# The adapter's first products of three tiles as split f16 parts, placed three steps later

## The reference, cut to what matters

```python
g = jnp.einsum('bsd,edf->ebsf', h, Wg)
u = jnp.einsum('bsd,edf->ebsf', h, Wu)
expert_outs = jnp.einsum('ebsf,efd->ebsd', jax.nn.silu(g) * u, Wd)
...
x = x + moe
h = jax.nn.relu(jnp.einsum('bsh,bha->bsa', x, w1) + b1)     # a = 32
adapted = jnp.einsum('bsa,bah->bsh', h, w2) + b2
out = x + layernorm(x + adapted) * gamma + beta
```

## Time and profile before

| | |
|---|---|
| median of 3 runs | 297.31 us (297.27 to 297.92) |
| profiled execution, its own time | 297.04 us |
| its span, first to last instruction | 295.2 us |
| PE busy / DVE busy / ACT busy | 290.1 / 268.8 / 231.1 us |
| granted TensorE clock, mean | 0.999 |

### The profile page before, as it was taken

The page is one execution under the profiler, slowest core; times in us unless marked ns, Lnnn a source line. Parts: engine busy times, 40 slices in busy tenths (PEclk is TensorE's granted clock), DMA queues, the critical chain, the costliest instruction groups (busy, mean ns, idle before and its releaser), DMA issues.

```text
span 295.2 us, 5086 instructions
## 1 busy us (share of the span) xinstructions
PE 290.1 (98%) x1510; PEld 144.3 (49%) x1510; DVE 268.8 (91%) x585; ACT 231.1 (78%) x517; POOL 19.3 (7%) x32
## 2 busy tenths in 40 slices
PE   8999999999999999999999999999999999999995
PEld 2444444444444444444444444444444444588883
DVE  5999999998989898988989999999999999977795
ACT  6998878788878787877897788887878876667771
POOL 3200201100000000000002010001100011000011
PEclk9999999999999999999999999999999999999999
DMA  6973110244000000000011001010001110000001
GB/s 208 385 307 109 52 65 19 62 120 112 2 2 0 0 2 0 0 2 1 1 22 26 18 9 39 12 25 19 17 3 39 27 18 10 2 36 3 0 2 36
DMA packets 17940, 13.39 MB, mean 45 GB/s; under 512 B 11486, under 2 KB 15994, under 8 KB 17914
## 3 DMA queue, kind: packets, MB, share of 16 engines
q1 hardware_dynamic: 17482, 12.86, 14.4%
q10 hardware_dynamic: 432, 0.21, 0.2%
HBM read 11.23 MB, written 1.05 MB: 42 GB/s over the span
## 4 chain that ended last, share of the span: by engine, by line
PE 94%; DVE 2%; DMA 1%; SPq 1%; issue 1%; ACT 0%; POOL 0%; POOLq 0%; DVEq 0%
PE moe_ps L449 10%; PE moe_ps L446 10%; PE moe_ps L447 10%; PE gate_ps L400 10%; PE up_ps L426 10%; PE up_ps L431 10%; PE up_ps L423 10%; PE gate_ps L403 10%; PE gate_ps L408 10%; DMA w_full<-weights 1%; DVE hidden L680 1%; PE adapt_ps L458 0%; DVE gx_lo L649 0%; SPq L319 0%; DVE h_lo L686 0%
## 5 line engine op out<-in xcount | busy, mean ns | idle before, releaser
L563 ACT ACTIVATE silu<-gate_ps 128x512 f32<-128x512 f32 (+1 forms) x160 | 88.2, 551 | 45.3 <-PE gate_ps L408 44.3
L680 DVE SCALAR_TENSOR_TENSOR hidden<-silu,up_ps 128x512 f32<-128x512 f32 (+1 forms) x160 | 100.3, 627 | 19.2 <-PE up_ps L431 11.6
L686 DVE TENSOR_TENSOR h_lo<-hidden,h_hi 128x512 f16<-128x512 f32 (+1 forms) x160 | 102.4, 640 | 0.2
L568 ACT ACTIVATE h_hi<-hidden 128x512 f16<-128x512 f32 (+1 forms) x160 | 92.8, 580 | 9.2 <-DVE hidden L680 8.4
L426 PE MATMUL up_ps<-gx_lo,w_hi 128*128 128x512 f16 (+1 forms) x160 | 57.3, 358 | 0.4 <-DVE gx_lo L649 0.4
L400 PE MATMUL gate_ps<-x_hi,w_hi 128*128 128x512 f16 (+1 forms) x160 | 57.4, 359 | 0.0
L431 PE MATMUL up_ps<-gx_hi,w_lo 128*128 128x512 f16 (+1 forms) x160 | 57.3, 358 | 0.0
L423 PE MATMUL up_ps<-gx_hi,w_hi 128*128 128x512 f16 (+1 forms) x160 | 57.3, 358 | 0.0
L403 PE MATMUL gate_ps<-x_lo,w_hi 128*128 128x512 f16 (+1 forms) x160 | 57.3, 358 | 0.0
L446 PE MATMUL moe_ps<-h_hi,w_hi 128*128 128x512 f16 (+1 forms) x160 | 57.3, 358 | 0.0
L449 PE MATMUL moe_ps<-h_lo,w_hi 128*128 128x512 f16 (+1 forms) x160 | 57.3, 358 | 0.0
(11 more groups left out here) (88 smaller groups left out, 148.6 us busy)
## 6 DMA issues: line engine op xcount, KB each, us to landing
w_full<-weights SPq DMA_DIRECT2D x8, 768.0 KB, 9.2
affine_sb<-affine SPq DMA_DIRECT2D x16, 128.0 KB, 2.9
x_full<-xT SPq DMA_DIRECT2D x3, 256.0 KB, 8.6
x<-x_blocks SPq DMA_DIRECT2D x48, 16.0 KB, 1.8
out_dram<-result SPq DMA_DIRECT2D x3, 256.0 KB, 2.1
w_full<-weights SPq DMA_DIRECT2D x4, 128.0 KB, 3.0
w_full<-w2b SPq DMA_DIRECT2D x24, 16.0 KB
w_full<-weights SPq DMA_DIRECT2D x1, 256.0 KB, 3.8
```

The source lines that it names most:

```text
L563: nc.scalar.activation(silu_slot(n), gate_ps[n % 2][:, 0:STEPS[n][4]], ACT.Silu, scale=1.0 / W_SCALE).then_inc(silu_ready, 1)
L568: nc.scalar.activation(h_slot(h_hi, n), hidden_slot(n), ACT.Copy).then_inc(h_hi_ready, 1)
L680: nc.vector.scalar_tensor_tensor(out=hidden_slot(n), in0=silu_slot(n), scalar=HIDDEN_RESCALE, in1=up_ps[n % 2][:, 0:STEPS[n][4]], op0=ALU. ...
L686: nc.vector.tensor_tensor(h_slot(h_lo, n), hidden_slot(n), h_slot(h_hi, n), ALU.subtract).then_inc(h_lo_ready, 1)
```

## The change

For jobs 0, 1 and 2 `adapter_in` no longer multiplies f32 x2T by f32 w1. ACT makes `w1_hi` (w1 times 64, 128x128) at `at` and `x2T_hi` (128x512) at `at`+1; DVE makes `w1_lo` at `at`+1 and `x2T_lo` at `at`+2. `adapter_in` then issues twelve f16 products (w1_hi·x_hi, w1_lo·x_hi, w1_hi·x_lo, four column groups each) and stands at `at`+4 instead of `at`+1. `adapter_relu` divides by 64 and follows at `at`+5, `h_upper` at `at`+6. `w2_upper` goes from `at` to `at`+2, `w2_lower` from `at`+2 to `at`+4, `h_others` from `at`+4 to `at`+7, `adapter_back` from `at`+6 to `at`+9, and y with all that follows it three steps later too (`stats_at` is counted from `back_at`). `moe_out` waits for the last `x2T_lo` in place of the last `adapter_in`.

```diff
 def in_at(j):
-    return 1 if j < MOVED else 2
+    return 4 if j < MOVED else 2
 def back_at(j):
-    return 6
+    return 9 if j < MOVED else 6
...
             def adapter_in(j):
                 t, first, count, _ = JOBS[j]
+                if j > 0:
+                    pe.wait_ge(y_ready, BEFORE[j])
+                if j < MOVED:
+                    pe.wait_ge(w1_lo_ready, j + 1)
+                    pe.wait_ge(x2T_lo_ready, j + 1)
+                    for of_w, of_x in ((w1_hi, x2T_hi), (w1_lo, x2T_hi), (w1_hi, x2T_lo)):
+                        for q in range(BATCHES):
+                            last = nc.tensor.matmul(fourth(adapt_ps, q)[:, 0:S], cols(of_w, q, A), cols(of_x, q, S),
+                                                    start=of_w is w1_hi and of_x is x2T_hi, stop=of_x is x2T_lo,
+                                                    tile_position=(0, q * A))
+                    last.then_inc(adapt_done, 1)
+                    return
...
+            def w1_upper(j):
+                act.wait_ge(adapter_loaded, adapter_count(JOBS[j][0]))
...
+                nc.scalar.activation(w1_hi[:, :], w1_sb[:, :], ACT.Copy, scale=W_SCALE).then_inc(w1_hi_ready, 1)
+
+            def x2T_upper(j):
+                act.wait_ge(x2T_ready, j + 1)
...
+                nc.scalar.activation(x2T_hi[:, :], x2T[:, :], ACT.Copy).then_inc(x2T_hi_ready, 1)
...
+            def w1_lower(j):
+                dve.wait_ge(w1_hi_ready, j + 1)
+                nc.vector.scalar_tensor_tensor(out=w1_lo[:, :], in0=w1_sb[:, :], scalar=W_SCALE, in1=w1_hi[:, :],
+                                               op0=ALU.mult, op1=ALU.subtract).then_inc(w1_lo_ready, 1)
+
+            def x2T_lower(j):
+                dve.wait_ge(x2T_hi_ready, j + 1)
+                nc.vector.tensor_tensor(x2T_lo[:, :], x2T[:, :], x2T_hi[:, :], ALU.subtract).then_inc(x2T_lo_ready, 1)
...
                 if since == 1 and j < MOVED:
                     turn_blocks(j)
+                if since == 1 and j < MOVED:
+                    w1_lower(j)
                 if since == 2 and j < MOVED:
+                    x2T_lower(j)
+                if since == 4 and j < MOVED:
                     w2_lower(j)
-                if since == 4 and j < MOVED:
+                if since == 7 and j < MOVED:
                     h_others(j)
```

More of the change, by code:

```diff
@@ L183, in build @@
         w2_stack = sb("w2_stack", [STACK, BATCHES * D], F16)
+        w1_hi = sb("w1_hi", [P, BATCHES * A], F16)
+        w1_lo = sb("w1_lo", [P, BATCHES * A], F16)
+        x2T_hi = sb("x2T_hi", [P, N], F16)
+        x2T_lo = sb("x2T_lo", [P, N], F16)
         x2 = sb("x2", [P, N], F32)
@@ L253, in build @@
         w2_lower_ready = sem("w2_lower_ready")
+        w1_hi_ready = sem("w1_hi_ready")
+        w1_lo_ready = sem("w1_lo_ready")
+        x2T_hi_ready = sem("x2T_hi_ready")
+        x2T_lo_ready = sem("x2T_lo_ready")
         tail_h_ready = sem("tail_h_ready")
@@ L452, in adapter_in @@
                 t, first, count, _ = JOBS[j]
+                if j > 0:
[10 more added lines that the diff above has]
+                    return
                 pe.wait_ge(x2T_ready, j + 1)
                 pe.wait_ge(adapter_loaded, adapter_count(t))
-                if j > 0:
-                    pe.wait_ge(y_ready, BEFORE[j])
                 for q in range(first, first + count):
@@ L460, in adapter_in @@
                 last.then_inc(adapt_done, 1)
-                if j < MOVED:
-                    return
                 pe.wait_ge(consts_ready, 1)
@@ L576, in adapter_relu @@
                         nc.scalar.activation(cols(h_full, q, S, A), fourth(adapt_ps, q)[:, 0:S], ACT.Relu,
-                                             bias=fourth(b1_sb, q)[:, 0:1]).then_inc(h_full_ready, 1)
+                                             bias=fourth(b1_sb, q)[:, 0:1],
+                                             scale=1.0 / W_SCALE).then_inc(h_full_ready, 1)
                     else:
@@ L580, in adapter_relu @@
                                              bias=fourth(b1_sb, q)[:, 0:1]).then_inc(adapt_h_ready, 1)
+            def w1_upper(j):
+                act.wait_ge(adapter_loaded, adapter_count(JOBS[j][0]))
+                if j > 0:
+                    act.wait_ge(adapt_done, j)
+                nc.scalar.activation(w1_hi[:, :], w1_sb[:, :], ACT.Copy, scale=W_SCALE).then_inc(w1_hi_ready, 1)
+            def x2T_upper(j):
+                act.wait_ge(x2T_ready, j + 1)
+                if j > 0:
+                    act.wait_ge(adapt_done, j)
+                nc.scalar.activation(x2T_hi[:, :], x2T[:, :], ACT.Copy).then_inc(x2T_hi_ready, 1)
             def w2_upper(j):
-                act.wait_ge(adapter_loaded, adapter_count(JOBS[j][0]))
                 if j > 0:
@@ L627, in _ @@
                     if n == at and j < MOVED:
+                        w1_upper(j)
+                    if n == at + 1 and j < MOVED:
+                        x2T_upper(j)
+                    if n == at + 2 and j < MOVED:
                         w2_upper(j)
@@ L691, in moe_out @@
                 if j > 0:
-                    dve.wait_ge(adapt_done, j)
+                    dve.wait_ge(x2T_lo_ready, min(j, MOVED))
                     dve.wait_ge(blocks_ready, j)
```

## The result

The changed kernel takes 298.38 us (median of 12 executions, 298.04 to 299.06), the kernel before 297.60 in the same rounds (12 executions, 297.09 to 298.27). The ratio is 1.0031, 95% interval 1.0021 to 1.0041: slower by 0.3%, 0.6 to 1.2 us. I had forecast 297.3 us and no change; the time lies inside my range, 296.7 to 298.5, and above my likeliest case, which ended at 297.8.

The account below looks back on a forecast made before the run. PE was taken to bound the kernel, with DVE narrowly keeping up. 297.04 - 0.05 (products) + 0.1 (PE waiting) = 297.1 us, 297.35 on the median's side; forecast 297.3 us, no change, range 296.7 to 298.5.

Parts of the forecast that it names:

- The block on PE: Adapter_in's products on PE: twelve f16 products cost 0.445 us against 0.46 for f32, so -0.05 us for three jobs.
- Entry: Start of the down product to the first adapter_in product on PE: 0.31 us as before, hole at the border kept.
- the rounds: Adapter_in's three rounds of four f16 products on PE: distance taken as 0.085 us, 0.17 for two.
- the last round to the gate product: End of adapter_in's block on PE: 0.22 us at most, taken as 0.17 for the shorter streaming.
- The first rival: Adapter_in on PE: the twelve products run one after another, +1.2 us for three jobs, 298.5 us; chance 0.11.
- the third: Rival at adapter_in's borders on PE: holes were due to f32 and go, -0.9 us, 296.4 us; chance 0.07.
- I allow 0.1 us of PE waiting over three jobs: Allowance for PE waiting on DVE, whose added 0.87 us a job was to be carried partly as lateness: 0.1 us.
- the 0.16 to 0.95 us that I gave x2T_lo of job 2: Forecast margin between the end of x2T_lo on DVE and PE's need of it at job 2's adapter_in.
- my lower number: Margin from hidden(113) to up(115) at job 2: 0.38 us if older results come on top, otherwise 1.17.
- Jobs 0 and 1 start with fewer old results or none before them: DVE's backlog at job starts: claimed lighter than at job 2, where three older parts took 0.79 us.
- the second rival: DVE lateness passes the two steps, PE waits at hidden or x2T_lo: +0.6 to +1.2 us, 298.2 us; chance 0.14.
- My sign for it: Test for the second rival: PE's waits for x2T_lo or hidden in steps 71 to 125 total above 0.6 us.

Follow-up runs that it names:

- e2: Kernel before with only the later places of the changed kernel, f32 products and no split parts: 297.63 us, ratio 1.0002.
- e6: Changed kernel with w1_lo and x2T_lo made on 32 columns only, the rest zeroed at the start: 297.69 us, ratio 0.9993.
- e7: Kernel before plus two DVE instructions a job like w1_lo and x2T_lo, outputs unread: 298.34 us, ratio 1.0026.
- e1: Changed kernel with POOL's x_beta also waiting for adapter_back of its job: 299.19 us, ratio 1.0056.
- e4: Changed kernel with adapter_back and all behind it one step later, at+10: 299.45 us, ratio 1.0059.
- e5: Changed kernel with the two h_others instructions in the other order, two-input one first: 299.44 us, ratio 1.0056.
- e9: Changed kernel with x_beta waiting for the second statistic of its job, about at+13: 298.24 us, ratio 1.0024.
- e11: Changed kernel with the plain copy of h_others made on ACT at at+7, behind that step's silu and h_hi: 297.45 us, ratio 0.9993.
- e12: As e11, with x_beta also waiting for the second statistic as in e9: 297.53 us, ratio 0.9993.

## Why the prediction was wrong

- **The block on PE** was right in kind and a little dear: 0.39 us, against 0.445 taken and 0.385 as the lower bound. Entry 0.31 as taken; the rounds lie 0.06 apart, by the width of the f16 stream and not near the f32 round; the last round to the gate product took 0.16. Gain 0.22 us instead of 0.05. (From the down product to the gate product it is 0.59 us, a hundredth under the 0.6 to 0.8 that I had named.) The first rival, one after another, and the third, no holes at the borders, are refuted by the same rows: 0.09 us still passes on entry, now with f16 on both sides of the border. TensorEngine Tiling (Key Properties) of the Trainium skill says that changing the tiling mode drains the engine; these 0.09 us agree with it.
- **The step that failed** is "I allow 0.1 us of PE waiting over three jobs". It was 1.17. The idle times that I had read, 1.1 and 0.4 us against 0.87 added, said that the work doesn't fit; I then let two steps of lateness carry it. In the runs it is 0.77 us against 2.23 and 0.83 of idle time at the later places (e2), which in the second stretch leaves next to nothing either. e6 and e7 show that this work is the cause, by taking it out and by adding it to the kernel before.
- **Where it showed.** I looked for it at up and adapter_in of job 2. There the margins held, if barely: of the 0.16 to 0.95 us that I gave x2T_lo of job 2 about 0.2 was left (it ended at 230.63 + 0.68 = 231.31 us, PE was there at 231.30 + 0.215 = 231.51), and 0.38, my lower number, at up(115). It showed at adapter_back of job 1, which I had priced at nothing, since "h_others and adapter_back keep their distance of two steps". A kept distance is a kept margin only if what stands ahead of h_others is not later, and this margin was small from the start: in the kernel before h_others ended at 154.42 + 0.68 = 155.10 us and adapter_back began at 155.57, 0.47 us later, and in jobs 1 and 2 it was 0.47 and 0.49. Nor did "Jobs 0 and 1 start with fewer old results or none before them" hold for job 1. Job 0's results fall into the steps 89 to 92, so job 1 starts with as many as job 2. The lines of the kernel before (h_others) and of the changed one (job 2):

```profile
154.42 0.68 DVE L713 SCALAR_TENSOR_TENSOR h_stack<-h_full,h_stack 32x512 f16<-32x512 f32 x1
...
229.00 0.25 DVE L733 SCALAR_TENSOR_TENSOR w_lo<-w_sb,w_hi 128x128 f16<-128x128 f32 x1
229.17 0.67 DVE L713 SCALAR_TENSOR_TENSOR hidden<-silu,up_ps 128x512 f32<-128x512 f32 x1
...
230.63 0.68 DVE L738 TENSOR_TENSOR x2T_lo<-x2T,x2T_hi 128x512 f16<-128x512 f32 x1
231.23 0.68 DVE L713 SCALAR_TENSOR_TENSOR hidden<-silu,up_ps 128x512 f32<-128x512 f32 x1
...
231.30 0.38 PE L458 MATMUL moe_ps<-h_lo,w_hi 128*128 128x512 f16 x1
```

- **x_beta** was misread. I noted that y left it behind and called that help. It now stood at h_others, whose result PE needs two steps later, where y's is needed by no product before the next job's adapter_in. I named this under the second rival and did not work it out.
- **The second rival** is nearest to what happened: its 0.6 to 1.2 us hold the 0.9 found, and its chance of 0.14 was too low. That its number fits is in part luck. It priced 0.2 to 0.4 us at hidden or x2T_lo in each of two or three jobs, and the profile of the changed kernel has one wait, at h_others in job 1. My sign for it, waits for x2T_lo or hidden above 0.6 us, would have denied it: there were none.
- **ACT** costs nothing by its added parts: e6 has them all and no waits. The weight loads caused none either.

## What to carry to other kernels

When a change adds to an engine off the critical path about as much work in a stretch as it has idle time there, a slot of two steps between producer and consumer only chooses which consumer pays. Take the idle time from the places where the work will stand, read each consumer's margin (from the end of what it needs to its own start, 0.47 us at adapter_back before the change) and price the wait at each, the small margins first. Moving the wait (e1, e4, e5, e9) does not cure it; moving half a microsecond of work a job to an engine with room, at a place where it delays nothing, does (e11, e12). A change that saves 0.07 us a block on the bound engine is not worth 0.77 us on the next one, if that has no room for it.

## What the runs showed of the hardware

One x_beta on POOL (128x512, two inputs) holds up one DVE instruction in each of the three jobs of every run, and which one is a matter of order: an h_lo took up to 1.56 us in the kernel before, h_others' two-input instruction 1.67 in the changed one. I had not expected the one-input copy of e5 to be held as well (1.38 for 0.42 us). hidden, which reads one operand from PSUM, is not held, here with x_beta in e9 running from 250.69 to 251.96 us:

```profile
251.09 0.69 DVE L713 SCALAR_TENSOR_TENSOR hidden<-silu,up_ps 128x512 f32<-128x512 f32 x1 [0.37 <-PE up_ps L440]
251.70 0.82 DVE L719 TENSOR_TENSOR h_lo<-hidden,h_hi 128x512 f16<-128x512 f32 x1
```

SBUF — State Buffer (Who interferes with whom) of the Trainium skill says the same: DVE and GpSimd share a port pair that is locked for a whole instruction by whichever comes first, taken by DVE instructions with two SBUF inputs where GpSimd reads SBUF too, as x_beta does, and by `tensor_scalar` in a two-port mode. The rows agree on both kinds (that e5's copy runs in such a mode no row shows, only that it was held), and in e5 and e6 the waiting goes the other way, with x_beta at 1.49 and 1.53 us instead of 1.27.
